# An AdaLN feed-forward kernel on one Trainium2 core: LoRA merge by three products of split operands, transfers and the first tile's y in another order

## The chip, the cores and the metric

The kernel runs on one core of one Trainium2 chip. The metric is the device time of one execution in microseconds (us), median of several runs. PE is TensorE, PEld its weight loads, DVE VectorE, ACT ScalarE, POOL GpSimd, SP the engine that here only issues transfers.

## The reference: what is computed

`x` holds 32 samples of 64 channels by 1024 values. Two residual layers follow each other:

```python
# layer 0: a 64x64 matrix per sample, chosen by its id, then a linear layer with eight LoRA adapters merged
y = jnp.einsum('bct,bcd->bdt', x, L0_cond_weights[itok_B_0_15])
h = jnp.einsum('bsd,nrd->nbsr', y, lora_A)                       # 8 adapters of rank 16
lora_out = jnp.einsum('nbsr,nor->bso', h, lora_B * (2 * lora_weights)[:, None, None])
x = x + jnp.einsum('bsd,od->bso', y, W) + bias + lora_out         # W is 1024 x 1024
# layer 1: a rank 16 adapter chosen by the sample's id, then a gated unit with 4-bit weights
v = jnp.einsum('bnr,bor->bno', jnp.einsum('bni,bri->bnr', x, B[ids]), A[ids])
inter = silu(v @ Wg.T) * (v @ Wu.T)                               # 2752 wide, weights from codes and scales
x = x + inter @ Wd.T
```

## The kernel before

The 2048 rows of `x` are 16 tiles of 128. All data is float32. Where a product has to be fast, both operands are split into a high part of the type fp32r and the rest (hi, lo), and three products are summed: hi by hi, hi by lo, lo by hi. An fp32r product of 512 columns is one pass on PE; a plain float32 product is shown in the trace as two records. The 4-bit codes of the second layer's weights are decoded all through the kernel: for each unit of 128 by 1024 codes ACT makes eight lines (L521, L525) in a ring of five buffers, DVE merges them into `val` in seven steps (L692, L694), multiplies by the scales (L711), PE turns the result (`turn_unit`), and ACT takes it out of PSUM (`evac_unit`).

Each engine's program is written out by hand and runs in its order; semaphores join them. Three stages follow each other:

**Setup** (0 to 48 us). The LoRA adapters are merged into W: We = W + B A, eight columns `jc` of 128 inputs. SP's queue loads the first unit's codes (`load_codes(0)`), then the eight columns of W with other inputs between them. ACT's queue loads `lb` (LoRA B), `lw` (the adapter weights) and `la` (LoRA A), all with the semaphore `lora_in`. DVE waits for all three, scales `lb` and puts it in order as `lbq`; PE turns it into `ps_t`; ACT copies it to `lbt`, which lies in the third buffer of `xs` (L586). Per column PE turns W (`turn_w`, eight transposes, L861) into one of two PSUM buffers (`ps_z` and `ps_gu` in turn, a column waits until the column two before it has been taken out) and adds the LoRA product with two plain float32 matmuls (`add_lora`, L866). ACT then writes `we_hi` (`evac_w`, L582) and DVE `we_lo` (`low_w`, L720). Between these stand decode work: ACT does 2 lines before each of the first four `evac_w` and 1 before the others, DVE 2 steps before each of the first two `low_w` and 1 before the others. After column 6 PE makes y of the first tile (`cond_y(0)`). After column 7 ACT takes y out (`evac_y`, both halves), DVE makes its low part (`low_y`, L744, both halves), and PE starts the tiles when `we_lo_ready` has counted all eight columns.

**Phase A** (16 tiles). Per tile PE computes z = y We by two halves of the output, each in two parts of four columns of y (`ffn_z`, L886, 12 matmuls a part), the y of the next tile, the turned sum x1 of the tile before (`turn_x1`, L895), the products of the adapters, and one or two turned units. The order in tile 0 is: z half 0 (both parts), y of tile 1, `turn_unit` of unit 0, z half 1 part 0, a bias product, `adapter_ga` of unit 0, z half 1 part 1, `turn_unit` of unit 1, then tile 1 with z half 0 part 0 and `turn_x1(0)`. DVE does in tile 0: 4 decode steps, `sum_x1` of half 0 (L751), 5 steps, `low_y` of tile 1's first half, 2 steps with the bias copy between them, then `low_y` of the second half and `sum_x1` of half 1, for which `turn_x1(0)` waits. ACT does 7 lines, `evac_unit(0)`, 2 lines, `evac_y`, 2 lines, `evac_ga(0)`, `evac_unit(1)` and then `evac_y` of tile 1's second half.

**Groups.** Six groups of hidden chunks, 16 slots each, compute the gated unit and add to the output in DRAM by accumulating transfers from POOL.

The functions below are those that the change touches and their callers.

Of the kernel before, what the change touches and what calls it, by code (L numbers as in the profile page):

```python
# [51 lines left out]
def adaln_ffn(nc, x, cond_id, adapter_id, cond_w, lora_a, lora_b, w0, bias0, lora_w, ad_a, ad_b,  # L52
# [3 lines left out]
    P = 128  # L56
# [90 lines left out]
    with ExitStack() as ctx:  # L147
# [52 lines left out]
        lbq = wt[:, 1, :, :]  # L200
        lbt = xs[:, XS - 1, :]
        ad_araw = x1t[:, :, :]
# [17 lines left out]
        ad_ids_in = sem("ad_ids_in")  # L220
        lora_in = sem("lora_in")
        ad_b_in = sem("ad_b_in")
# [18 lines left out]
        ad_at_ready = sem("ad_at_ready")  # L241
        lb_scaled = sem("lb_scaled")
        setup_t = sem("setup_t")
        setup_evac = sem("setup_evac")
# [84 lines left out]
        def _(sp):  # L329
# [20 lines left out]
            def load_x(t):  # L350
                slot = t % XS
                if t == XS - 1:
                    sp.wait_ge(we_mm, DC)
                elif t >= XS:
                    sp.wait_ge(x1t_mm, t - XS + 1)
                    sp.wait_ge(x1_out[slot], 16 * (t // XS))
                sp.dma_start(xs[:, slot, :], x_rows[t * P:(t + 1) * P, :]).then_inc(x_in[slot], 16)
# [5 lines left out]
            def load_w(jc):  # L363
                sp.dma_start(w_stage[jc][:, :, :], w0.rearrange("(q p) j -> p q j", p=P)[:, :, jc * P:(jc + 1) * P]
                             ).then_inc(w_in[jc], 16)

            load_codes(0)
            for jc in range(3):
                load_w(jc)
            sp.dma_start(ad_braw[:, :], ad_b.rearrange("n r d -> (n r) d")).then_inc(ad_b_in, 16)  # L370
# [139 lines left out]
        def _(act):  # L510
            act.dma_start(lb, lora_b.rearrange("n (p q) r -> p n (q r)", p=P)).then_inc(lora_in, 16)
            act.dma_start(lw[:, :], lora_w.partition_broadcast(P)).then_inc(lora_in, 16)
            act.dma_start(la[:, :], lora_a.rearrange("n r d -> (n r) d")).then_inc(lora_in, 16)
            def line(n, k):
# [65 lines left out]
            def evac_w(jc):  # L580
                act.wait_ge(we_mm, jc + 1)
                act.activation(we_hi[:, jc, :], ps_w[jc % 2][:, :], ACT.Copy).then_inc(we_hi_ready, 1)  # L582

            some_lines(0, 3)
            act.wait_ge(setup_t, 1)
            act.activation(lbt.rearrange("j (p q) -> j q p", q=DC),  # L586
                           ps_t[:, :].rearrange("j (q p) -> j q p", q=DC), ACT.Copy).then_inc(setup_evac, 1)
            at = 3
            for jc in range(DC):
                some_lines(at, 2 if jc < 4 else 1)  # L590
                at += 2 if jc < 4 else 1
                evac_w(jc)
                if jc == 4:
                    act.wait_ge(setup_t, 2)
                    act.wait_ge(ad_at_ready, 1)
                    act.activation(ad_bt[:, :, :].rearrange("p q t -> p (q t)"), ps_t[:, :], ACT.Copy
                                   ).then_inc(setup_evac, 1)
            evac_y(0, 0)
            evac_y(0, 1)
            some_lines(at, 1)  # L600
# [75 lines left out]
        def _(dve):  # L676
# [62 lines left out]
            def low_y(t, part):  # L739
                qs = slice(part * DC // 2, (part + 1) * DC // 2)  # L740
                dve.wait_ge(y_hi_ready, 2 * t + part + 1)
                if t == 0:
                    dve.wait_ge(we_mm, DC)
                dve.tensor_tensor(y_lo[:, qs, :].rearrange("p q t -> p (q t)"), ps_y[:, part * HALF:(part + 1) * HALF],  # L744
# [8 lines left out]
            def mask_bx(t):  # L753
# [6 lines left out]

            dve.wait_ge(lora_in, 16 * 3)
            dve.tensor_scalar(lw[:, :], lw[:, :], LORA_SCALE, None, ALU.mult).then_inc(lw_ready, 1)
# [3 lines left out]
            dve.tensor_copy(lbq.rearrange("p q (n r) -> p q n r", n=NAD),  # L766
                            lb.rearrange("p n (q r) -> p q n r", q=DC)).then_inc(lb_scaled, 1)
            some_steps(0, 2)
            at = 2
            for jc in range(DC):  # L770
                some_steps(at, 2 if jc < 2 else 1)
                at += 2 if jc < 2 else 1
                low_w(jc)
                if jc == 3:
                    dve.wait_ge(ad_a_in, 16)
                    dve.tensor_copy(ad_at[:, :, :, :], ad_araw.rearrange("p n (q r) -> p q n r", q=DC)
                                    ).then_inc(ad_at_ready, 1)
# [8 lines left out]
            assert at == STEPS_SETUP  # L786
            low_y(0, 0)
            low_y(0, 1)
            dve.wait_ge(mask_step, 3)

# [65 lines left out]
        def _(pe):  # L856
# [7 lines left out]
            def add_lora(jc):  # L864
                for h in range(2):
                    ins = pe.matmul(ps_w[jc % 2][:, h * HALF:(h + 1) * HALF], la[:, jc * P:(jc + 1) * P],  # L866
                                    lbt[:, h * HALF:(h + 1) * HALF], start=False, stop=True)
                ins.then_inc(we_mm, 1)
# [10 lines left out]
            def ffn_z(t, h, part):  # L879
                half = slice(h * HALF, (h + 1) * HALF)  # L880
                pe.wait_ge(y_lo_ready, 2 * t + part + 1 if h == 0 else 2 * (t + 1))
                if part == 0:
                    wait(pe, x1_ready, 2 * (t - 1) + h + 1)
# [54 lines left out]
            turn_w(1)  # L938
            pe.wait_ge(setup_evac, 1)
            add_lora(0)  # L940
# [12 lines left out]
            pe.wait_ge(ad_at_ready, 1)  # L953
            pe.wait_ge(we_lo_ready, DC)
            for t in range(NT):
# [104 lines left out]
```

## Time and profile before

| | us |
|---|---|
| median of 3 runs | 1100.68 (1100.24 to 1100.74) |
| the profiled execution's own time | 1100.7 |
| its span, first to last instruction | 1099.0 |
| PE busy | 1026.5 (93%) |
| DVE busy, ACT busy | 813.6 (74%), 806.4 (73%) |
| setup, until the first z matmul | 47.9 |
| end of phase A's last z matmul | about 356 |

The views of the profile give for each instruction its start and duration on its engine, and the idle time before it with what ended that. A group "x3" is several instructions run together. The granted clock (PEclk) is the share of TensorE's full clock in a stretch: 1.00 is 2.4 GHz, 0.50 is 1.2 GHz.

### The profile page before, as it was taken

What the parts mean: (1) busy time and instruction counts of PE and PEld (TensorE: products, weight loads), DVE (VectorE), ACT (ScalarE), POOL (GpSimd) and SP (SyncE); (2) the same over time, 40 slices, a digit from 0 to 9 for tenths busy, and PEclk for the clock granted to TensorE, in tenths of its full rate; (3) what the DMA queues carried; (4) which work ended last, traced back from release to release, by engine and by line L of the source; (5) the groups of instructions that cost most, each with busy time, mean ns of one, the idle gap of its engine ahead of it and who ended that gap; (6) DMA issues with size and microseconds to landing.
All of it is one profiled execution on the core that took longest, in us unless ns stands there. A gap on an engine that the chain in (4) does not pass through costs nothing.

```text
span 1099.0 us, 14511 instructions
## 1 busy us (share of the span) xinstructions
PE 1026.5 (93%) x5352; PEld 861.5 (78%) x5352; DVE 813.6 (74%) x815; ACT 806.4 (73%) x961; POOL 213.1 (19%) x285
## 2 busy tenths in 40 slices
PE   4899999999999889899999999999989999899995
PEld 3588888988888767778778778787878877788884
DVE  4778887878787788778888888888887788871220
ACT  4767777776677788878888888888888888863341
POOL 4003223232221111111111111121111211122111
PEclk9899999999999998999999999999999999999998
DMA  9735444464342366565645446455554645534667
GB/s 245 220 96 137 102 124 116 109 154 110 85 98 58 58 115 111 100 115 96 115 82 92 96 96 115 97 95 96 102 100 87 116 80 103 106 58 68 107 114 115
DMA packets 62950, 117.89 MB, mean 107 GB/s; under 512 B 6272, under 2 KB 38544, under 8 KB 62880
## 3 DMA queue, kind: packets, MB, share of 16 engines
q0 software_dynamic: 17504, 59.80, 34.7%
q1 hardware_dynamic: 44048, 56.11, 17.7%
q10 hardware_dynamic: 1328, 1.05, 0.3%
q8 instruction: 43, 0.70, 0.3%
q14 instruction: 27, 0.22, 0.1%
HBM read 58.22 MB, written 67.11 MB: 114 GB/s over the span
## 4 chain that ended last, share of the span: by engine, by line
PE 54%; DVE 24%; ACT 10%; issue 9%; SPq 2%; DMA 1%; DVEq 0%; POOL 0%; ACTq 0%
DVE val L692 12%; PE ps_z L1009 12%; PE ps_y L1009 11%; PE ps_z L886 10%; PE ps_gu L991 6%; DVE val L694 5%; ACT ring L525 5%; PE ps_t L928 3%; PE ps_t L920 3%; PE ps_gu L928 3%; ACT inter L629 2%; PE ps_y L875 2%; PE ps_gu L903 2%; DVE val L711 1%; DVE wd_late_lo L736 1%
## 5 line engine op out<-in xcount | busy, mean ns | idle before, releaser
L525 ACT ACTIVATE ring<-codes 128x1024 f32<-128x1024 int32 x455 | 455.4, 1053 | 119.2 <-DVE val L692 114.5
L692 DVE TENSOR_TENSOR val<-val,ring 128x1024 f32<-128x1024 f32 x260 | 318.1, 1223 | 15.2 <-issue 0.2
L694 DVE SCALAR_TENSOR_TENSOR val<-ring,val 128x1024 f32<-128x1024 f32 x195 | 238.0, 1220 | 11.1 <-ACT ring L525 2.5
L819 DVE TENSOR_TENSOR inter<-ps_gu,inter 128x512 f32<-128x512 f32 x88 | 60.7, 690 | 149.6 <-ACT inter L629 149.6
L497 POOL DMA_DIRECT2D out<-staged x96 | 82.6, 860 | 379.0 <-ACT staged L643 375.1
L886 PE MATMUL ps_z<-we_hi,y_hi 128*128 128x512 f32 x256 | 105.5, 412 | 3.6 <-DVE y_lo L744 3.6
L886 PE MATMUL ps_z<-we_hi,y_lo 128*128 128x512 f32 x256 | 101.1, 395 | 0.0
L886 PE MATMUL ps_z<-we_lo,y_hi 128*128 128x512 f32 x256 | 100.9, 394 | 0.0
L629 ACT ACTIVATE inter<-ps_gu 128x512 f32<-128x512 f32 x88 | 51.7, 587 | 62.9 <-PE ps_gu L991 62.3
L920 PE MATMUL ps_t<-ident,val 128*128 128x128 f32 x520 | 70.9, 280 | 20.0 <-DVE val L711 19.1
L1009 PE MATMUL ps_y<-wd_late_hi,in_hi 128*128 128x512 f32 x256 | 82.1, 402 | 6.9 <-DVE in_lo L825 5.5
L920 PEld LDWEIGHTS ps_t<-ident,val 128*128 128x128 f32 x520 | 64.5, 175 | 30.1 <-DVE val L711 24.5
L436 POOL TENSOR_TENSOR st_hi<-ga_f,one 128x128 fp32r<-128x128 f32 x42 | 28.7, 683 | 294.3 <-ACT ga_f L565 294.1
L1009 PE MATMUL ps_z<-wd_late_hi,in_hi 128*128 128x512 f32 x256 | 81.1, 398 | 0.0
L635 ACT ACTIVATE in_hi<-inter 128x512 fp32r<-128x512 f32 x88 | 55.5, 631 | 34.3 <-DVE inter L819 34.3
L521 ACT ACTIVATE val<-codes 128x1024 f32<-128x1024 int32 x65 | 68.7, 1057 | 9.1 <-PE ps_t L920 4.8
L1009 PE MATMUL ps_y<-wd_late_lo,in_hi 128*128 128x512 f32 x240 | 74.7, 393 | 0.0
L1009 PE MATMUL ps_y<-wd_late_hi,in_lo 128*128 128x512 f32 x240 | 74.5, 392 | 0.0
L1009 PE MATMUL ps_z<-wd_late_lo,in_hi 128*128 128x512 f32 x240 | 74.1, 390 | 0.0
L1009 PE MATMUL ps_z<-wd_late_hi,in_lo 128*128 128x512 f32 x240 | 74.0, 389 | 0.0
L991 PE MATMUL ps_gu<-bx_hi,st_hi 128*128 128x512 f32 x176 | 69.6, 395 | 3.5 <-DVE inter L819 3.5
L991 PE MATMUL ps_gu<-bx_hi,st_lo 128*128 128x512 f32 x176 | 69.6, 395 | 0.0
(117 smaller groups left out, 1829.8 us busy)
## 6 DMA issues: line engine op xcount, KB each, us to landing
out<-staged POOLq DMA_DIRECT2D x96, 512.0 KB, 5.3
codes<-in_L_ffn_gate_codes SPq DMA_DIRECT2D x21, 512.0 KB, 3.5
codes<-in_L_ffn_up_codes SPq DMA_DIRECT2D x21, 512.0 KB, 3.7
codes<-in_L_ffn_down_codes SPq DMA_DIRECT2D x21, 512.0 KB, 4.0
xs<-in_x SPq DMA_DIRECT2D x16, 512.0 KB, 3.6
out<-in_L_ffn_bias SPq DMA_DIRECT2D x4, 2048.0 KB, 13.2
out<-xs POOLq DMA_DIRECT2D x16, 512.0 KB, 5.5
w_stage<-in_L_ffn_W SPq DMA_DIRECT2D x8, 512.0 KB, 9.9
```

What stands on the lines that cost most here:

```text
L497: pool.dma_start(out_rows[t * P:(t + 1) * P, :], staged[:, place, :], accum_op=ALU.add).then_inc(acc_out[place], 16)
L521: act.activation(val_of(n), codes[:, n % 2, :], ACT.Relu, bias=offset, scale=slope).then_inc(lines, 1)
L525: act.activation(ring[:, (k - 1) % RING, :], codes[:, n % 2, :], ACT.Identity, bias=offset, scale=slope).then_inc(lines, 1)
L629: act.activation(inter[:, q % 2, :], ps_g[:, :], ACT.Silu).then_inc(silu_ready, 1)
L692: ins = dve.tensor_tensor(v, v, line, pick)
L694: ins = dve.scalar_tensor_tensor(out=v, in0=line, scalar=add, in1=v, op0=ALU.add, op1=pick)
L819: dve.tensor_tensor(inter[:, q % 2, :], ps_u[:, :], inter[:, q % 2, :], ALU.mult).then_inc(inter_ready, 1)
L886: ins = pe.matmul(ps_z[:, half], y[:, jc, :], w[:, jc, half], start=jc == 0 and p == 0, stop=jc == DC - 1 and p == 2)
L920: ins = pe.transpose(ps_t[:, q * P:(q + 1) * P], v[:, q, :], ident[:, :])
L928: ins = pe.matmul(ga_bank(n), ad_at[:, q, :, :].rearrange("p n r -> p (n r)"), wt[:, m % 2, q, :], start=q == 0, stop=q == DC - 1)
L991: ins = pe.matmul(ps, w[:, c % ST, m, :], v[:, cols], start=p == 0, stop=p == 2)
L1009: ins = pe.matmul(ps_o[slot % 2][:, h * HALF:(h + 1) * HALF], v[:, b % 2, k, s * P:(s + 1) * P], wd_of(c, w)[:, h * HALF:(h + 1) * HALF], ...
```

## The change

- `lbt` and `la` are split into hi and lo parts. These lie in `bx_hi` and `bx_lo`, which phase A fills later; `lbt` leaves `xs`. ACT makes `la_hi` (a copy as soon as `la` has come) and `lbt_hi`, both ahead of its first three decode lines. DVE makes `la_lo` and `lbt_lo` ahead of its first two decode steps. `add_lora` takes six fp32r matmuls of 512 columns in place of two float32 ones, and PE waits for both low parts.
- DVE's first wait is for `lb` and `lw` alone; `la` has a semaphore of its own.
- SP loads columns 0 and 1 of W ahead of the first codes. The third tile's x no longer waits for the end of the merge.
- ACT's `evac_y` of tile 0 stands ahead of the last `evac_w`, DVE's `low_y` ahead of the last `low_w`, without its wait for the last column. PE starts z when seven columns of `we_lo` are done, and waits for the eighth ahead of each part 1.

```diff
@@ -198,7 +198,8 @@
 
         lb = wt[:, 0, :, :].rearrange("p (n q) r -> p n (q r)", n=NAD)
         lbq = wt[:, 1, :, :]
-        lbt = xs[:, XS - 1, :]
+        lbt_hi, la_hi = bx_hi[:, 0:D], bx_hi[:, D:2 * D]
+        lbt_lo, la_lo = bx_lo[:, 0:D], bx_lo[:, D:2 * D]
         ad_araw = x1t[:, :, :]
 
         in_hi = sb("in_hi", [P, 2, IN, HALF], F32R)
@@ -218,7 +219,8 @@
 
         ids_in = sem("ids_in")
         ad_ids_in = sem("ad_ids_in")
-        lora_in = sem("lora_in")
+        lora_a_in = sem("lora_a_in")
+        lora_b_in = sem("lora_b_in")
         ad_b_in = sem("ad_b_in")
         ad_a_in = sem("ad_a_in")
         bias_in = sem("bias_in")
@@ -240,6 +242,8 @@
         lw_ready = sem("lw_ready")
         ad_at_ready = sem("ad_at_ready")
         lb_scaled = sem("lb_scaled")
+        la_hi_ready = sem("la_hi_ready")
+        lora_lo_ready = sem("lora_lo_ready")
         setup_t = sem("setup_t")
         setup_evac = sem("setup_evac")
         we_mm = sem("we_mm")
@@ -349,9 +353,7 @@
 
             def load_x(t):
                 slot = t % XS
-                if t == XS - 1:
-                    sp.wait_ge(we_mm, DC)
-                elif t >= XS:
+                if t >= XS:
                     sp.wait_ge(x1t_mm, t - XS + 1)
                     sp.wait_ge(x1_out[slot], 16 * (t // XS))
                 sp.dma_start(xs[:, slot, :], x_rows[t * P:(t + 1) * P, :]).then_inc(x_in[slot], 16)
@@ -364,9 +366,10 @@
                 sp.dma_start(w_stage[jc][:, :, :], w0.rearrange("(q p) j -> p q j", p=P)[:, :, jc * P:(jc + 1) * P]
                              ).then_inc(w_in[jc], 16)
 
+            load_w(0)
+            load_w(1)
             load_codes(0)
-            for jc in range(3):
-                load_w(jc)
+            load_w(2)
             sp.dma_start(ad_braw[:, :], ad_b.rearrange("n r d -> (n r) d")).then_inc(ad_b_in, 16)
             load_w(3)
             sp.dma_start(ad_araw.rearrange("p (n q) r -> p n (q r)", n=NAD),
@@ -508,9 +511,9 @@
 
         @block.scalar
         def _(act):
-            act.dma_start(lb, lora_b.rearrange("n (p q) r -> p n (q r)", p=P)).then_inc(lora_in, 16)
-            act.dma_start(lw[:, :], lora_w.partition_broadcast(P)).then_inc(lora_in, 16)
-            act.dma_start(la[:, :], lora_a.rearrange("n r d -> (n r) d")).then_inc(lora_in, 16)
+            act.dma_start(lb, lora_b.rearrange("n (p q) r -> p n (q r)", p=P)).then_inc(lora_b_in, 16)
+            act.dma_start(lw[:, :], lora_w.partition_broadcast(P)).then_inc(lora_b_in, 16)
+            act.dma_start(la[:, :], lora_a.rearrange("n r d -> (n r) d")).then_inc(lora_a_in, 16)
             def line(n, k):
                 if n >= NU:
                     return
@@ -581,22 +584,25 @@
                 act.wait_ge(we_mm, jc + 1)
                 act.activation(we_hi[:, jc, :], ps_w[jc % 2][:, :], ACT.Copy).then_inc(we_hi_ready, 1)
 
+            act.wait_ge(lora_a_in, 16)
+            act.activation(la_hi, la[:, :], ACT.Copy).then_inc(la_hi_ready, 1)
+            act.wait_ge(setup_t, 1)
+            act.activation(lbt_hi.rearrange("j (p q) -> j q p", q=DC),
+                           ps_t[:, :].rearrange("j (q p) -> j q p", q=DC), ACT.Copy).then_inc(setup_evac, 1)
             some_lines(0, 3)
-            act.wait_ge(setup_t, 1)
-            act.activation(lbt.rearrange("j (p q) -> j q p", q=DC),
-                           ps_t[:, :].rearrange("j (q p) -> j q p", q=DC), ACT.Copy).then_inc(setup_evac, 1)
             at = 3
             for jc in range(DC):
                 some_lines(at, 2 if jc < 4 else 1)
                 at += 2 if jc < 4 else 1
+                if jc == DC - 1:
+                    evac_y(0, 0)
+                    evac_y(0, 1)
                 evac_w(jc)
                 if jc == 4:
                     act.wait_ge(setup_t, 2)
                     act.wait_ge(ad_at_ready, 1)
                     act.activation(ad_bt[:, :, :].rearrange("p q t -> p (q t)"), ps_t[:, :], ACT.Copy
                                    ).then_inc(setup_evac, 1)
-            evac_y(0, 0)
-            evac_y(0, 1)
             some_lines(at, 1)
             at += 1
             assert at == LINES_AT[0]
@@ -739,8 +745,6 @@
             def low_y(t, part):
                 qs = slice(part * DC // 2, (part + 1) * DC // 2)
                 dve.wait_ge(y_hi_ready, 2 * t + part + 1)
-                if t == 0:
-                    dve.wait_ge(we_mm, DC)
                 dve.tensor_tensor(y_lo[:, qs, :].rearrange("p q t -> p (q t)"), ps_y[:, part * HALF:(part + 1) * HALF],
                                   y_hi[:, qs, :].bitcast(F32).rearrange("p q t -> p (q t)"), ALU.subtract
                                   ).then_inc(y_lo_ready, 1)
@@ -758,18 +762,28 @@
                                          in1=mask[:, PER * t:PER * (t + 1)].unsqueeze(2).to_broadcast([P, PER, CH]),
                                          op0=ALU.add, op1=ALU.mult).then_inc(bx_masked, 1)
 
-            dve.wait_ge(lora_in, 16 * 3)
+            dve.wait_ge(lora_b_in, 16 * 2)
             dve.tensor_scalar(lw[:, :], lw[:, :], LORA_SCALE, None, ALU.mult).then_inc(lw_ready, 1)
             dve.wait_ge(lw_ready, 1)
             dve.tensor_tensor(lb, lb, lw[:, :].unsqueeze(2).to_broadcast([P, NAD, P]), ALU.mult).then_inc(lw_ready, 1)
             dve.wait_ge(lw_ready, 2)
             dve.tensor_copy(lbq.rearrange("p q (n r) -> p q n r", n=NAD),
                             lb.rearrange("p n (q r) -> p q n r", q=DC)).then_inc(lb_scaled, 1)
+            dve.wait_ge(la_hi_ready, 1)
+            dve.tensor_tensor(la_lo, la[:, :], la_hi.bitcast(F32), ALU.subtract).then_inc(lora_lo_ready, 1)
+            dve.wait_ge(setup_evac, 1)
+            dve.tensor_tensor(lbt_lo.rearrange("j (p q) -> j q p", q=DC),
+                              ps_t[:, :].rearrange("j (q p) -> j q p", q=DC),
+                              lbt_hi.bitcast(F32).rearrange("j (p q) -> j q p", q=DC), ALU.subtract
+                              ).then_inc(lora_lo_ready, 1)
             some_steps(0, 2)
             at = 2
             for jc in range(DC):
                 some_steps(at, 2 if jc < 2 else 1)
                 at += 2 if jc < 2 else 1
+                if jc == DC - 1:
+                    low_y(0, 0)
+                    low_y(0, 1)
                 low_w(jc)
                 if jc == 3:
                     dve.wait_ge(ad_a_in, 16)
@@ -784,8 +798,6 @@
             dve.wait_ge(ad_ids_in, 16)
             dve.tensor_scalar(mask[:, :], ad_ids[:, :], part_f[:, 0:1], None, ALU.is_equal).then_inc(mask_step, 1)
             assert at == STEPS_SETUP
-            low_y(0, 0)
-            low_y(0, 1)
             dve.wait_ge(mask_step, 3)
 
             for t in range(NT):
@@ -863,8 +875,10 @@
 
             def add_lora(jc):
                 for h in range(2):
-                    ins = pe.matmul(ps_w[jc % 2][:, h * HALF:(h + 1) * HALF], la[:, jc * P:(jc + 1) * P],
-                                    lbt[:, h * HALF:(h + 1) * HALF], start=False, stop=True)
+                    half = slice(h * HALF, (h + 1) * HALF)
+                    for p, (a, b) in enumerate(((la_hi, lbt_hi), (la_hi, lbt_lo), (la_lo, lbt_hi))):
+                        ins = pe.matmul(ps_w[jc % 2][:, half], a[:, jc * P:(jc + 1) * P], b[:, half],
+                                        start=False, stop=p == 2)
                 ins.then_inc(we_mm, 1)
 
             def cond_y(t):
@@ -879,6 +893,8 @@
             def ffn_z(t, h, part):
                 half = slice(h * HALF, (h + 1) * HALF)
                 pe.wait_ge(y_lo_ready, 2 * t + part + 1 if h == 0 else 2 * (t + 1))
+                if part == 1:
+                    pe.wait_ge(we_lo_ready, DC)
                 if part == 0:
                     wait(pe, x1_ready, 2 * (t - 1) + h + 1)
                 for jc in range(part * DC // 2, (part + 1) * DC // 2):
@@ -936,7 +952,7 @@
                 ins = pe.transpose(ps_t[:, q * P:(q + 1) * P], lbq[:, q, :], ident[:, :])
             ins.then_inc(setup_t, 1)
             turn_w(1)
-            pe.wait_ge(setup_evac, 1)
+            pe.wait_ge(lora_lo_ready, 2)
             add_lora(0)
             add_lora(1)
             for jc in range(2, DC):
@@ -951,7 +967,7 @@
                     cond_y(0)
             pe.wait_ge(setup_evac, 2)
             pe.wait_ge(ad_at_ready, 1)
-            pe.wait_ge(we_lo_ready, DC)
+            pe.wait_ge(we_lo_ready, DC - 1)
             for t in range(NT):
                 a, b, b_before = PLACE_A[t, 0], PLACE_A.get((t, 1)), PLACE_A.get((t - 1, 1))
                 ffn_z(t, 0, 0)
```

## Rows read from the trace of the kernel before

**Rows 1.** The page, part 1: busy time, share of the span, instructions of each engine.

```profile
PE 1026.5 (93%) x5352; PEld 861.5 (78%) x5352; DVE 813.6 (74%) x815; ACT 806.4 (73%) x961; POOL 213.1 (19%) x285
```

**Rows 2.** Stretches: length, busy time (count) by engine, PEclk, DMA share, GB/s.

```profile
24.00:36.00 12.00, 10.50 (x52) 6.28 (x51) 9.48 (x10) 9.21 (x10) 0.00 (x0) 1.00 1.10 319
...
44.00:48.00 4.00, 0.42 (x2) 0.16 (x1) 2.55 (x6) 3.31 (x5) 0.00 (x0) 0.81 0.32 121
...
48.00:54.00 6.00, 6.00 (x16) 4.70 (x17) 5.13 (x5) 3.60 (x4) 0.00 (x0) 0.56 0.48 175
...
80.00:120.00 40.00, 40.00 (x248) 35.54 (x247) 34.31 (x35) 30.49 (x36) 11.01 (x16) 1.00 0.58 144
```

**Rows 3.** The chain that ended last, 0 to 120 us: start, us, what.

```profile
19.46 8.60 DMA codes<-in_L_ffn_up_codes
...
30.09 1.23 DVE we_lo L720
...
31.46 1.06 PE ps_z L861 x8
...
32.52 1.72 PE ps_z L866 x4
...
42.57 1.73 PE ps_gu L866 x4
...
47.87 8.23 PE ps_z L886 x24
...
86.27 5.46 PE ps_z L886 x24
```

**Rows 4.** Timeline, setup: start, us, engine line op out<-in [idle before <-what ended it].

```profile
11.92 1.94 PE L861 MATMUL ps_z<-ident,w_stage 128*128 128x128 f32 x8 [11.92 <-DMA w_stage<-in_L_ffn_W]
...
12.56 0.17 DVE L762 TENSOR_SCALAR lw<-lw 128x8 f32<-128x8 f32 x1 [12.56 <-DMA la<-in_L_ffn_lora_A]
...
16.78 2.04 ACT L586 ACTIVATE xs<-ps_t 128x1024 f32<-128x1024 f32 x1 [8.44 <-PE ps_t L936]
...
18.87 2.10 PE L866 MATMUL ps_z<-xs,la 128*128 128x512 f32 x4 [0.42 <-ACT xs L586]
...
35.77 1.22 DVE L720 TENSOR_TENSOR we_lo<-ps_z,we_hi 128x1024 fp32r<-128x1024 f32 x1
```

**Rows 5.** Transfers issued at 0.87 (codes) and 1.78 us (W column 1): KB, us to landing.

```profile
codes<-in_L_ffn_gate_codes SPq DMA_DIRECT2D x1, 512.0 KB, 4.5
...
w_stage<-in_L_ffn_W SPq DMA_DIRECT2D x1, 512.0 KB, 14.4
```

**Rows 6.** Timeline, end of setup and tile 0.

```profile
47.04 1.28 DVE L744 TENSOR_TENSOR y_lo<-ps_y,y_hi 128x512 fp32r<-128x512 f32 x2
...
47.63 1.06 ACT L521 ACTIVATE val<-codes 128x1024 f32<-128x1024 int32 x1 [0.37 <-DMA codes<-in_L_ffn_gate_codes]
...
52.15 1.23 DVE L711 TENSOR_TENSOR val<-val,gu_scales 128x1024 f32<-128x1024 f32 x1
...
56.75 3.87 DVE L694 SCALAR_TENSOR_TENSOR val<-ring,val 128x1024 f32<-128x1024 f32 x3
...
66.41 1.06 ACT L525 ACTIVATE ring<-codes 128x1024 f32<-128x1024 int32 x1 [0.29 <-DVE val L692]
...
68.76 1.03 ACT L537 ACTIVATE wt<-ps_t 128x1024 f32<-128x1024 f32 x1 [1.12 <-PE ps_t L920]
...
71.64 1.09 PE L895 MATMUL ps_t<-ident,xs 128*128 128x128 f32 x8 [0.17 <-DVE xs L751]
```

**Rows 7.** Timeline of PE in the groups, where it stood idle before a step.

```profile
624.35 1.16 PE L920 MATMUL ps_t<-ident,val 128*128 128x128 f32 x8 [2.10 <-DVE val L711]
...
714.45 2.90 PE L928 MATMUL ps_t<-wt,ad_at 128*128 128x128 f32 x16 [1.87 <-ACT wt L537]
```

**Rows 8.** Stretches around these two.

```profile
624.00:628.00 4.00, 3.65 (x20) 3.07 (x20) 3.17 (x4) 4.00 (x6) 0.00 (x0) 1.00 0.03 4
...
714.00:720.00 6.00, 5.55 (x25) 4.97 (x26) 5.86 (x7) 5.35 (x8) 0.06 (x1) 0.72 0.32 87
```

## The prediction

> **What bounds the kernel now.** First the page's busy times: PE works 93% of the span and no other engine over 74% [rows 1], so time is won where PE stands still or runs slowly. The stretches tell where. In phase A PE is busy 40.00 of 40 us at the upper clock, DVE 34.31 [rows 2]; PE bounds it, and whatever moves the start of the tiles moves the end. From 44 to 48 us PE works only 0.42 us, and from 48 to 54 its granted clock is 0.56 on the mean [rows 2]: the hole at the end of setup and the lower of the two levels (1.2 GHz) behind it. Third, the chain of waits: the last LoRA product ends at 44.30 (42.57 and 1.73), ACT and DVE finish the last column and then make the low part of y, and z starts at 47.87 [rows 3]. Its first 24 matmuls take 8.23 us where 24 later ones take 5.46 [rows 3]. So 3.57 us are a wait and 2.77 us the clock after it. I call the end of the last LoRA product L; before, L is 44.30.
>
> The same chain shows what holds the front of setup: the second unit's codes, issued at 19.46, land 8.60 later at 28.06. ACT then makes one line and `evac_w(2)`, DVE's `low_w(2)` follows at 30.09, and column 4 is turned at 31.46 [rows 3]. Everything earlier is worth only what it does to this.
>
> **The front of setup: gains nothing.** DVE started at 12.56, when `la` came [rows 4]; now `lb` and `lw` free it. But three other things come later. Ahead of the first lines ACT has `la_hi` (not before 12.6; about 1.03 by [rows 6], ACT at 68.76) and `lbt_hi` (2.04 [rows 4]), ending at about 15.7; it was idle 8.44 us here [rows 4], which pays for both. The first codes now stand third on SP's queue, behind 1 MB of W. Before, the third transfer there (column 1 of W) landed 14.4 us after its issue at 1.78, so at 16.2, and the codes at 5.4 [rows 5]. The same three transfers in another order put the codes at no later than about 16.2; I take 16.2. ACT then does five lines (1.06 each [rows 6]) to 21.5, `evac_w(0)` (1.03 like the eviction there) to 22.5, two lines, `evac_w(1)` to 25.7 and line 7 to 26.7: 1.3 us before the codes that it needs next, which keep their place behind the same bytes on the same queue. DVE has `la_lo` (1.22 as [rows 4], DVE at 35.77) and `lbt_lo`. The trace has no DVE write with that step: at least 1.22, and if the step doubles it as it doubled ACT's (2.04 against 1.03) 2.44; I take 1.22, the same operation. Either end is over by 18.3, when DVE's first step gets its second line, so it costs nothing. From 18.3 DVE does four steps, `low_w(0)`, two steps, `low_w(1)` and a step: 7 times 1.23 and 2 times 1.22 [rows 4, 6] give 29.4, against `low_w(2)` at 30.09. So column 4 is again turned at about 31.5, with 0.7 us to spare on DVE. If the first codes or `la` come more than that later, each us beyond is a us on L.
>
> **The columns: 0 to 1.4 us.** `add_lora` falls from 1.72 [rows 3] to six matmuls of 5.46/24 = 0.228 each, 1.37: 0.35 less per column. Not all of it counts: for columns 5 and 6 PE waits for DVE, whose `low_w(4)` starts at 35.77 because DVE comes from other work [rows 4]. That leaves columns 6 and 7: L = 44.30 - 0.70 = 43.6 (bounds: nothing, 44.3; all of columns 4 to 7, 42.9). Against it stands the clock. PE now ends `add_lora(1)` by 20 to 22 us and must wait for `low_w(0)` until about 24.4, so a hole of 2 to 4 us. Holes in this trace: 3.57 us was followed by the lower level [rows 2, 3], 1.87 too, 2.10 was not [rows 7, 8]. At the lower level column 2 takes 1.94 (eight transposes at 11.92 [rows 4]) and twice 1.37, so to 29.1, and column 4 is turned 1.4 us later; of that about 0.65 reaches L, as the columns behind have slack in their waits for DVE. With even chances I put L at **43.9** (43.6 to 44.3).
>
> A rule speaks against this part. The chain has eight transposes per column at 1.06 with the clock up from 24 to 36 us [rows 2, 3]; and after nothing but transposes since 11.92 the first LoRA matmuls at 18.87 ran nearly at the rate of later ones (2.10 for four against 1.72) [rows 3, 4]. The Trainium skill, "TensorE: Matmul & The Clock Gate", Part 4, says that in transpose mode the full clock does not engage, as it doesn't count as PE-busy in the same way. By that rule, with less matmul time between the transposes, the merge would run at the lower level; the trace disagrees, since transposes alone brought the clock up. What this would cost is the slower rival below.
>
> **The end of setup: the main gain, and what is late next.** `evac_y` and `low_y` now finish while PE turns and merges the last column, so z can start at L + 0.1, with PE never idle and the clock up. The wait for the eighth column ahead of part 1 is met: `evac_w(7)` and `low_w(7)` take 1.03 and 1.22 after L [rows 4, 6], 2.3 with their handoffs, and part 0 has 12 matmuls, 2.73. In later tiles this wait is met long before; it costs 32 satisfied waits, and where z's parts with one and two waits follow each other now, 24 matmuls run at 0.228 without a step [rows 3], so nothing. If PE alone counted, it would come to `turn_x1(0)` 0.1 + (71.64 - 0.17 - 47.87 - 2.77) = 20.9 us after L [rows 3, 6].
>
> But DVE and ACT are next. `turn_x1(0)` needs `sum_x1`, which stands behind all of DVE's and ACT's work of tile 0. Before, from L to `turn_x1(0)` it was 71.64 - 44.30 = 27.34 [rows 3, 6]. Out of this falls: `low_y`, moved ahead of L, 1.28 (at 47.04); DVE's wait for z, from 53.38 (52.15 and 1.23) to 56.10 (47.87 and 8.23), 2.72; and ACT's wait for PE ahead of `evac_unit(1)`, 1.12 [rows 3, 6]. The rest stays, for it is DVE steps back to back (from 56.75 to 66.41, where ACT's line waits for the last of them) and then ACT, DVE and PE in turn. I add 0.3, because ACT's seven lines, one eviction and two lines in tile 0 now end a little after DVE wants the y behind them (0 to 1). So 27.34 - 1.28 - 2.72 - 1.12 + 0.3 = 22.5 after L: 1.6 later than PE alone. Of the third unit's codes ACT has use at 47.63, their landing [rows 6]; its next line then waits for DVE until about L + 5.2 = 49.1, so this isn't the limit while L is above 43.5.
>
> **The sum.** `turn_x1(0)` comes at 43.9 + 22.5 = 66.4 instead of 71.64: 5.2 us. At that point all engines stand to each other as before (ACT behind `evac_y`, DVE behind `sum_x1`), and every later wait is for another engine or a transfer issued by one, so the shift stays. The profiled execution took 1100.7, as the median does (1100.68): **1095.5**. The bounds of L (42.9 to 44.3) and of the 0.3 give 1093.8 to 1096.6.
>
> **The rivals.** (a) DVE is not next, or does its tile 0 quicker than here: PE's path alone, 43.9 + 20.9 = 64.8, gain 6.8, 1093.9. For it: PE's 93% [rows 1]; against: the steps back to back. (b) One more fall of the clock. PE gets a new hole of about 1.6 us at `turn_x1(0)`, and the holes in the groups move against the clock's decisions: 1.87 cost a fall, 2.10 did not [rows 7, 8]. One fall costs about what it did at 48 us, 2.77 [rows 3]: 1098.3. (c) The same luck the other way, one fall fewer: 1092.7. (d) The front is late by more than its slack, by some 3 to 5 us (first codes or `la` landing late, so that ACT and DVE lag): L is 47 to 49 and the gain 0 to 2: 1099 to 1101, the case in which the moves only shift the wait. (e) Slower: the whole merge at the lower clock level, because transposes with shorter products between them, or the holes ahead of each column, let it stay down. A column is then 1.94 + 2.74 = 4.7 [rows 3, 4]; six from 24.4, with the adapter's eight transposes and the 16 records of y between them (three times 1.94, an estimate), put L at 58.4, 14.1 later than before, and the 4.9 won behind L shrink to about 3.5 as z starts slowly too: 1100.7 + 10.6 = 1111. The page's rule would have it so. It decides from L = 71.64 - 22.5 = 49.1 on, that is when more than about two and a half columns behind column 3 run so, each 2.3 us over. Against it: at the lower level PE is itself the last to finish, without holes, and after 47.87 the clock came back within six us of work [rows 2].
>
> **How the numbers follow.** The forecast 0.52, (a) 0.10, (b) 0.15, (c) 0.10, (d) 0.08, (e) 0.05. A measurement of this kernel can tell about 0.2%, 2.2 us, from no change. Faster by that (under 1098.5): the forecast, (a), (c) and over half of (b), 0.83. Slower: (e), 0.05. Within: 0.12. A range from 1092.2 to 1098.8 holds the forecast, (a), (c) and most of (b), and leaves (d) and (e) out.
>
> **What will show it.** Column 4 turned at about 31.5 (up to 33 with the clock down); the merge's end at 43.6 to 44.3; the first z within 0.3 us of it, and its 24 matmuls in 5.5 us; `turn_x1(0)` near 66.4 with PE idle about 1.5 us before it, released by DVE; from there a constant shift against the kernel before. It is wrong if z waits for `y_lo` or the eighth column, if the first codes land after 17 us and column 4 moves with them, if the clock is down beyond 33 us, or if the shift changes in the groups.

## The result and the profile after

The changed kernel took 1094.19 us (median of five runs, 1092.53 to 1096.04) against 1100.68 us: a ratio of 0.9943, 95% interval 0.9929 to 0.9958. The forecast was 1095.5. The profiled execution took 1094.19, with a span of 1092.5.

The chain of waits of the kernel after, in order of time (start, us, what), answers to [rows 3]:

```profile
18.61 8.93 DMA codes<-in_L_ffn_up_codes
...
36.60 1.07 PE ps_z L873 x8
...
41.72 1.40 PE ps_gu L880 x6
...
64.66 0.61 DVE xs L755
...
65.31 1.09 PE ps_t L911 x8
```

The second unit's codes still hold the front: they land at 27.54, before at 28.06. The six matmuls of a column take 1.40 (four records of float32 took 1.72). The merge ends at L = 41.72 + 1.40 = 43.12, before at 44.30. `turn_x1(0)` is now at 65.31 instead of 71.64, released by DVE.

The timeline shows the front, z's start and the end of tile 0 (start, us, instruction, in brackets the idle time before it and what ended it), beside [rows 4, 6]:

```profile
10.78 1.06 ACT L588 ACTIVATE bx_hi<-la 128x1024 fp32r<-128x1024 f32 x1 [6.87 <-DMA la<-in_L_ffn_lora_A]
...
14.79 2.01 DVE L775 TENSOR_TENSOR bx_lo<-ps_t,bx_hi 128x1024 fp32r<-128x1024 f32 x1 [1.69 <-ACT bx_hi L590]
...
15.10 1.06 ACT L524 ACTIVATE val<-codes 128x1024 f32<-128x1024 int32 x1 [0.34 <-DMA codes<-in_L_ffn_gate_codes]
...
17.14 3.89 DVE L700 SCALAR_TENSOR_TENSOR val<-ring,val 128x1024 f32<-128x1024 f32 x3 [0.33 <-ACT ring L528]
...
23.63 1.94 PE L873 MATMUL ps_z<-ident,w_stage 128*128 128x128 f32 x8 [2.42 <-DVE we_lo L726]
...
27.34 1.04 PE L873 MATMUL ps_gu<-ident,w_stage 128*128 128x128 f32 x8
...
27.56 1.06 ACT L524 ACTIVATE val<-codes 128x1024 f32<-128x1024 int32 x1 [2.96 <-DMA codes<-in_L_ffn_up_codes]
...
30.93 1.06 PE L873 MATMUL ps_z<-ident,w_stage 128*128 128x128 f32 x8 [0.29 <-DVE we_lo L726]
...
43.26 0.47 PE L902 MATMUL ps_z<-we_hi,y_hi 128*128 128x512 f32 x1
...
58.10 0.68 DVE L748 TENSOR_TENSOR y_lo<-ps_y,y_hi 128x512 fp32r<-128x512 f32 x1
...
65.31 1.09 PE L911 MATMUL ps_t<-ident,xs 128*128 128x128 f32 x8 [0.96 <-DVE xs L755]
```

The stretches at the end of setup (length, busy time by engine, granted clock, DMA) answer to the middle rows of [rows 2]:

```profile
44.00:48.00 4.00, 4.00 (x19) 3.27 (x18) 3.59 (x6) 2.19 (x3) 0.00 (x0) 1.00 0.51 164
...
48.00:54.00 6.00, 6.00 (x40) 5.41 (x39) 5.76 (x6) 5.15 (x6) 0.00 (x0) 1.00 0.21 81
```

PE is busy 4.00 of 4 us where it had 0.42, and the clock is 1.00 where it was 0.81 and 0.56. z starts 0.14 us after the merge. What is left of the hole is the 0.96 us of idle PE ahead of `turn_x1(0)`, and DVE ends it.

Behind `turn_x1(0)` the two profiles take the same time: the span's end comes 1092.5 - 65.31 = 1027.2 us later, before 1099.0 - 71.64 = 1027.4. So the shift of 6.3 us made in setup and tile 0 is the whole difference of the two spans but 0.2. That they agree so closely is partly chance: in the other profiles below this stretch takes 1026.3 to 1029.0 us.

### The profile page after: what moved, and what is told of

It reads as the page before. It is cut to its first block, busy times and chain, and to the rows that moved or that the text cites. A ratio compares the mean times of both kernels' runs of the same rounds, so it can differ in the third digit from the quotient of the medians.

```text
span 1092.5 us, 14576 instructions
## 1 busy us (share of the span) xinstructions
PE 1023.8 (94%) x5368; PEld 864.8 (79%) x5368; DVE 816.8 (75%) x817; ACT 807.1 (74%) x962; POOL 213.1 (20%) x285
## 4 chain that ended last, share of the span: by engine, by line
PE 52%; DVE 26%; ACT 10%; issue 9%; SPq 2%; DMA 1%; DVEq 0%; POOL 0%; ACTq 0%
DVE val L698 13%; PE ps_z L1025 12%; PE ps_y L1025 11%; PE ps_z L902 9%; PE ps_gu L1007 6%; DVE val L700 6%; ACT ring L528 5%; PE ps_t L944 3%; PE ps_t L936 3%; PE ps_gu L944 3%; ACT inter L635 2%; PE ps_gu L919 2%; PE ps_y L889 2%; DVE val L717 2%; DVE wd_late_lo L742 1%
```

## Experiments

All were timed beside the kernel before on the same chip; there that kernel's medians were 1099.0 to 1100.3. T is the start of `turn_x1(0)`, L the end of the last LoRA product, both from each run's own profile.

| kernel | L | T | T - L | median us | ratio, 95% interval |
|---|---|---|---|---|---|
| before (first profile) | 44.30 | 71.64 | 27.3 | 1100.68 | |
| before again | 44.68 | 69.50 | 24.8 | 1099.06 | 0.9994 [0.9984, 1.0005] |
| after (first profile) | 43.12 | 65.31 | 22.2 | 1094.19 | 0.9943 [0.9929, 0.9958] |
| after again | 42.82 | 65.01 | 22.2 | 1094.07 | 0.9953 [0.9939, 0.9966] |
| y early alone | 44.50 | 66.70 | 22.2 | 1095.50 | 0.9962 [0.9947, 0.9976] |
| all but y early | 43.21 | 69.65 | 26.4 | 1097.86 | 0.9983 [0.9973, 0.9993] |
| codes first | 43.63 | 65.83 | 22.2 | 1094.77 | 0.9960 [0.9944, 0.9975] |
| before, clock held | 44.78 | 69.61 | 24.8 | 1098.28 | 0.9989 [0.9978, 1.0000] |
| after, hole filled | 44.71 | 66.90 | 22.2 | 1094.62 | 0.9952 [0.9938, 0.9965] |
| after, a step moved | 42.61 | 64.08 | 21.5 | 1091.15 | 0.9922 [0.9909, 0.9936] |
| after, masks early | 42.99 | 64.53 | 21.5 | 1093.01 | 0.9937 [0.9924, 0.9951] |
| after, both of these | 42.99 | 64.45 | 21.5 | 1091.81 | 0.9926 [0.9912, 0.9939] |
| after, ten steps in four tiles | 43.54 | 65.03 | 21.5 | 1090.97 | 0.9911 [0.9896, 0.9927] |

**One part alone.** The y split early, in the kernel before:

```diff
+                if jc == DC - 1:
+                    evac_y(0, 0)
+                    evac_y(0, 1)
                 evac_w(jc)
...
-                if t == 0:
-                    dve.wait_ge(we_mm, DC)
...
+                if jc == DC - 1:
+                    low_y(0, 0)
+                    low_y(0, 1)
                 low_w(jc)
...
+                if part == 1:
+                    pe.wait_ge(we_lo_ready, DC)
...
-            pe.wait_ge(we_lo_ready, DC)
+            pe.wait_ge(we_lo_ready, DC - 1)
```

> The kernel before with only the split y moved ahead of the last column (ACT, DVE and PE's two waits); LoRA stays in float32, transfers in their old order. Theory: the merge ends at 44.3 as before, z starts within 0.2 us of it at the upper clock, turn_x1(0) follows 22.2 us after the merge's end at 66.5 instead of 71.64, and the time falls by 5.1 us to about 1095.6. Rival (DVE is not next, PE alone sets tile 0): turn_x1(0) at 65.2, 1094.3. Rival (the gain is the cheaper merge's): 1100.7.

The changed kernel without that part (the same diff, undone):

> The changed kernel with the split y back behind the last column; split LoRA and the new transfers stay. Theory: the merge ends at 43.1, the hole of 3.6 us and the lower clock behind it come back, turn_x1(0) at 43.1 + 27.3 = 70.4, so 1.2 us under the kernel before: 1099.5. Rival (the merge's gain is lost because the second unit's codes and DVE set the columns): 1100.7. Rival (the split merge carries most of the gain): under 1097.

The chain of the first of them, and then of the second:

```profile
42.77 1.73 PE ps_gu L866 x4
...
66.70 1.09 PE ps_t L897 x8
```

```profile
41.82 1.39 PE ps_gu L880 x6
...
46.79 7.33 PE ps_z L900 x24
...
69.65 1.09 PE ps_t L909 x8
```

With y early alone the merge ends where it did, and T - L falls to 22.2: T stands at 66.70 where 66.5 was expected, not at the 65.2 of PE alone. Without it, L has its gain and the hole is back (z 3.58 us after L). So y early shortens what comes behind the merge, and the rest of the change moves the merge's end by about 1.2 us. Measured end to end, all but y early brought 1.2 us, as expected, and y early alone 3.5, not 5.1. The next experiment shows a reason: executions of the kernel before differ, and T of y early alone lies 4.9 us below the T of its first profile and 2.8 below that of its second.

**The clock by itself.** Fifteen matmuls that nobody reads are to hold the clock in the hole of the kernel before:

```diff
+            for _ in range(15):
+                pe.matmul(ps_t[:, 0:HALF], we_hi[:, 0, 0:P], we_hi[:, 0, 0:HALF], start=True, stop=True)
             pe.wait_ge(we_lo_ready, DC)
```

> The kernel before with 15 matmuls of 512 columns, whose result nobody reads, in the hole at the end of setup; z still waits for y and the last column until 47.9. Theory: the clock stays at its upper level, the first 24 z matmuls take 5.5 us instead of 8.2, and turn_x1(0) comes 2.8 us earlier (PE sets it: DVE's wait for z of 2.7 us goes): 1097.9. Rival (only the wait counts, the slow start hides beside DVE's steps): 1100.7.

And a second profile each of the two kernels, unchanged:

> The kernel before, for a second profile. Theory: turn_x1(0) at 71.6 if the clock is down for all of the first 13 z matmuls as in the first profile, up to 1 us earlier if it comes back sooner; the time behind turn_x1(0) is 1027 us as in every profile so far. Rival (the stages behind also differ from run to run by 1 us or more without the clock): another time behind it.

> The changed kernel, for a second profile and a comparison on one chip with the others. Theory: the merge's end at 43.1 to 43.6, turn_x1(0) 22.2 us later, 1027 us behind it; 5 to 6.3 us shorter than the kernel before on the same chip. Rival (the profile of the changed kernel was a lucky one): turn_x1(0) at 66.4 or later, 4 us or less.

The chain of the kernel with the clock held, then chain and stretches of the kernel before in its second profile:

```profile
48.36 5.72 PE ps_z L886 x24
...
69.61 1.09 PE ps_t L895 x8
```

```profile
48.25 5.72 PE ps_z L886 x24
...
69.50 1.09 PE ps_t L895 x8
...
44.00:48.00 4.00, 0.66 (x2) 0.00 (x0) 2.17 (x5) 3.15 (x5) 0.00 (x0) 1.00 0.29 107
...
48.00:54.00 6.00, 5.75 (x26) 4.81 (x27) 5.50 (x6) 3.40 (x4) 0.00 (x0) 1.00 0.52 175
```

With the fifteen matmuls z's first 24 take 5.72 instead of 8.23, and T - L is 24.8, 2.5 less than in the first profile (2.8 were expected). But the unchanged kernel shows the same 5.72 and the same 24.8 in its second profile: a hole as long as before (3.57 us), and no fall of the clock behind it (1.00, where [rows 2] have 0.81 and 0.56). So whether the clock falls in this hole differs from one execution to the next; behind the hole of 3.58 us in the kernel with all but y early it did fall (z took 7.33). That the fifteen matmuls hold the clock is therefore not shown by their profile; in the median they brought 0.8 us, and the interval reaches no difference. The times of the kernel before spread in the same sense: of its 26 executions beside this run, the three with a mean granted clock of 0.982 took 1102.5 to 1103.0 us, the two with 0.988 took 1097.6 and 1097.9. In which stretches these had the lower clock is not known. What y early takes out of T - L is 2.6 us in either case (24.8 to 22.2) and about 2.5 more in those executions in which the clock falls. From the second profile of before to the second of after T moves by 4.5 us, from the first to the first by 6.3.

Such a difference between executions stands behind T too. The second profile of the changed kernel has T at 65.01, but from there to the end it takes 1.8 us longer, and one stretch accounts for 1.6 of that. First the first profile, then the second, each with PE's next step behind the hole:

```profile
353.00:367.00 14.00, 11.56 (x64) 9.43 (x65) 8.77 (x12) 9.90 (x13) 0.86 (x2) 1.00 0.19 35
...
365.12 0.70 PE L1025 MATMUL ps_y<-wd_late_hi,in_hi 128*128 128x512 f32 x2 [1.33 <-DVE wd_late_lo L742]
```

```profile
353.00:367.00 14.00, 11.68 (x59) 9.81 (x60) 7.33 (x10) 8.71 (x12) 0.86 (x2) 0.88 0.17 33
...
366.40 0.70 PE L1025 MATMUL ps_y<-wd_late_hi,in_hi 128*128 128x512 f32 x2 [1.54 <-DVE wd_late_lo L742]
```

The last `turn_x1` comes at 353.41 and 353.09, with 1.08 us of idle PE before it and 0.70 behind it in both, and the step at the end of the stretch 11.7 and 13.3 us later: the clock fell in one and not in the other, for 1.6 us. In all profiles the time from T to the end is 1026.3 to 1029.0 us where the tiles' work is as in the kernel before; the tiles between, from the first `turn_x1` to the last, take 288.1 in both profiles of both kernels.

**The transfers' order.** The first codes ahead of W again:

```diff
+            load_codes(0)
             load_w(0)
             load_w(1)
-            load_codes(0)
             load_w(2)
```

> The changed kernel with the first codes again ahead of columns 0 and 1 of W. Theory: column 0 lands at 11.8 instead of 5.7, so the turned LoRA B and its split come some 2.7 us later, and with them ACT's lines and DVE's steps; 1.35 us of that are slack on DVE ahead of low_w(2), the rest, 1 to 1.4 us, goes on to the merge's end: 1095.2 to 1095.6. Rival (the front is all slack, the second unit's codes set it): 1094.2.

L is 43.63, 0.5 to 0.8 later than in the two profiles of the changed kernel. But L also moves with the landing of the second unit's codes, and that has to be taken out first. In six profiles of the new merge (six matmuls of split operands a column) ACT stands idle over 2 us until they land, and in each of them L comes 15.54 to 15.56 us after the start of ACT's first line on them (27.56 and 43.12 in the changed kernel's first profile). In the four profiles of the old merge it is 16.21 to 16.22 (28.09 and 44.30 in the first). So these codes set L, and the cheaper merge is worth 16.21 - 15.55 = 0.66 us; what else L gains is that they land earlier, with that line at 27.07 to 28.00 against 28.09 to 28.57. Why they do stays open. In this run:

```profile
27.67 1.06 ACT L524 ACTIVATE val<-codes 128x1024 f32<-128x1024 int32 x1 [0.80 <-DMA codes<-in_L_ffn_up_codes]
```

ACT is idle for 0.80 us only, and L is 15.96 behind: the old order costs 0.4 us on L. The theory had 1 to 1.4. The medians (1094.77 against 1094.07 and 1094.19) don't show a difference of this size.

**The hole ahead of column 2.** Sixteen matmuls that nobody reads, behind `add_lora(1)`:

```diff
             add_lora(1)
+            for _ in range(16):
+                pe.matmul(ps_t[:, 0:HALF], la_hi[:, 0:P], lbt_hi[:, 0:HALF], start=True, stop=True)
```

> The changed kernel with 16 matmuls of 512 columns, whose result nobody reads, in the hole ahead of column 2. Theory: the clock no longer falls there (0.50 from 24 to 26 us in the changed kernel), columns 2 and 3 take their short time, but the merge still ends at 43.1 to 43.3, since the second unit's codes at 27.6 and DVE set column 4: no difference in the median, though the spread of the runs may be smaller. Rival (the fall of the clock ahead of column 2 costs time on the path in most runs): 0.6 us or more shorter than the changed kernel beside it.

```profile
13.22 1.06 ACT L588 ACTIVATE bx_hi<-la 128x1024 fp32r<-128x1024 f32 x1 [9.31 <-DMA la<-in_L_ffn_lora_A]
...
23.62 4.18 PE L959 MATMUL ps_t<-bx_hi 128*128 128x512 f32 x16
...
27.63 1.04 PE L873 MATMUL ps_z<-ident,w_stage 128*128 128x128 f32 x8
...
33.02 1.04 PE L873 MATMUL ps_z<-ident,w_stage 128*128 128x128 f32 x8
```

This didn't test what it should. The filler held column 2 until 27.63, and ACT stood idle 2.12 us until it was merged; besides, `la` came 2.4 us later here than in the first profile. Column 4 was turned at 33.02 and L is 44.71. Two kernels of the next experiments settle what this one left open. In the one with the masks early `la` was as late (13.40), and L is 15.93 us behind ACT's line on the second unit's codes, 0.4 over the 15.55. Here it is 17.79 behind, 2.2 over, so most of that is the filler's own. And in the kernel with both changes the hole was 1.34 us long, and column 2's transposes ran at the upper rate behind it:

```profile
23.58 1.07 PE L873 MATMUL ps_z<-ident,w_stage 128*128 128x128 f32 x8 [1.34 <-DVE we_lo L726]
...
27.44 1.06 ACT L524 ACTIVATE val<-codes 128x1024 f32<-128x1024 int32 x1 [2.89 <-DMA codes<-in_L_ffn_up_codes]
```

Its L is 42.99, 15.55 behind that line, as in the changed kernel, where column 2's transposes ran at the lower rate (1.94). So the lower clock behind the hole ahead of column 2 costs nothing on L: even with it column 3's transposes start at 27.34, and the codes that ACT needs next land at 27.54, after them.

**What is next in tile 0.** One decode step and line of tile 0 goes to tile 12:

```diff
-    STEPS_A = [11 if t < 12 else 10 for t in range(NT)]
+    STEPS_A = [11 if 0 < t < 13 else 10 for t in range(NT)]
```

> The changed kernel with one of the 11 decode steps and lines of tile 0 moved to tile 12. Theory (DVE's steps of tile 0 set turn_x1(0), PE stands idle 0.96 us before it): the step of 1.23 us leaves the path, PE's idle time there falls to a few hundredths, and turn_x1(0) comes 0.9 us earlier, 64.4 with the merge's end at 43.1; the run is 0.9 us shorter than the changed kernel beside it. Rival (that idle time is covered elsewhere, or PE or ACT's eviction of unit 1 is next at the same point): no difference.

The three steps for the masks, to where DVE waits for `la_hi` (and, in another kernel, both changes):

```diff
+            dve.wait_ge(part_ready, 1)
...
+            dve.tensor_scalar(mask[:, :], ad_ids[:, :], part_f[:, 0:1], None, ALU.is_equal).then_inc(mask_step, 1)
             dve.wait_ge(la_hi_ready, 1)
```

> The changed kernel with the three small DVE steps of the masks (0.64 us from the end of low_w(7) to the first decode step of tile 0) moved to the start of DVE's program, where it waits for la_hi. Theory (DVE sets tile 0): turn_x1(0) comes 0.6 us earlier against the merge's end, 21.6 us instead of 22.2, PE's idle time ahead of it falls from 0.96 to about 0.35 us, the time behind it stays at 1027. Rival (PE or ACT is next at once): 22.1 to 22.2.

> The changed kernel with both: one decode step of tile 0 moved to tile 12, and the masks early. Theory: PE alone now sets tile 0 (20.9 to 21.2 us from the merge's end to turn_x1(0) by its own work), so against the step alone, which gave 21.5, the masks bring 0.2 to 0.3 us and no more; about 1091. Rival (DVE still sets it): 20.9.

The step in front of which PE stood idle, in the timelines of these three in their order:

```profile
64.08 1.09 PE L911 MATMUL ps_t<-ident,xs 128*128 128x128 f32 x8 [0.24 <-DVE xs L755]
```

```profile
64.53 1.09 PE L911 MATMUL ps_t<-ident,xs 128*128 128x128 f32 x8 [0.20 <-DVE xs L755]
```

```profile
64.45 1.09 PE L911 MATMUL ps_t<-ident,xs 128*128 128x128 f32 x8 [0.24 <-DVE xs L755]
```

Each takes about 0.7 us from T - L (22.2 to 21.5), PE's idle time falls from 0.96 to 0.2, and both together bring no more than one. What stands behind DVE's steps is in the chain of the kernel with the step moved:

```profile
60.21 0.89 PE ps_t L936 x8
...
62.05 0.60 ACT y_hi L574
...
63.34 0.69 DVE xs L755
```

PE turns unit 1, ACT takes it and then y out of PSUM, DVE makes `low_y` (for which it stood idle 3.25 us) and `sum_x1`: this series ends at 21.5 us after L, and PE's own work ahead of `turn_x1(0)` ends 0.24 us before that. The expected 0.2 to 0.3 us more from both changes didn't come. The step moved was expected to bring 0.9 us and brought 2.9 (1094.07 to 1091.15 on one chip). 0.7 of that are in tile 0; in the profiles 1.7 are in the tiles behind, 286.4 us from the first `turn_x1` to the last instead of 288.1. To see whether that was DVE's lag, ten steps in the first four tiles, eleven in all others:

```diff
-    STEPS_A = [11 if t < 12 else 10 for t in range(NT)]
+    STEPS_A = [10 if t < 4 else 11 for t in range(NT)]
```

> The changed kernel with 10 decode steps in tiles 0 to 3 and 11 in all others, instead of 11 in tiles 0 to 11 and 10 behind. Theory for tile 0: as with one step moved, 21.5 us from the merge's end to turn_x1(0). For phase A, where moving one step took 1.7 us out of the 288.1 between the first and the last turn_x1, if that was DVE's lag in the tiles: 286.4 or less. Rival (the order of the units was luck): 287 to 289, since tiles 12 to 15 now have a step more.

```profile
65.03 1.09 PE L911 MATMUL ps_t<-ident,xs 128*128 128x128 f32 x8 [0.24 <-DVE xs L755]
...
350.89 1.06 PE L911 MATMUL ps_t<-ident,xs 128*128 128x128 f32 x8 [1.08 <-DVE wd_early_lo L742]
```

285.9 us between the two rows, 2.2 under 288.1, with more steps in the last tiles. So where the decode steps stand sets part of phase A's time. How it does is read from PE between the first `turn_x1` and the last: the stretch (length, PE's busy time) and PE's waits there for DVE's `sum_x1` (us in total, times, longest), for the changed kernel, the step moved and the ten steps:

```profile
65.31:353.41 288.10, 282.48 (x1762) 249.54 (x1763) 235.12 (x236) 206.99 (x243) 71.13 (x108) 1.00 0.47 112
...
PE ps_t L911 <- DVE xs L755: 3.9, 8, 1.0
```

```profile
64.08:350.44 286.36, 282.04 (x1762) 249.62 (x1763) 236.22 (x237) 209.45 (x245) 72.77 (x108) 1.00 0.47 113
...
PE ps_t L911 <- DVE xs L755: 2.4, 7, 0.6
```

```profile
65.03:350.89 285.86, 282.23 (x1763) 249.73 (x1763) 236.06 (x237) 209.86 (x245) 77.23 (x108) 1.00 0.48 113
...
PE ps_t L911 <- DVE xs L755: 1.3, 5, 0.4
```

PE stands idle 5.6 us in the changed kernel, 4.3 with the step moved, 3.6 with the ten steps, and its work stays the same within 0.5. The stretch from 80 to 120 us [rows 2], where PE was busy 40.00 of 40 us, is not typical of the phase: most of the gain is time in which PE waited for DVE ahead of a `turn_x1`. With 1090.97 us this kernel has the lowest median, but it can't be told from the step alone (0.9911 and 0.9922, with intervals that overlap). Its interval lies below both of the changed kernel's, that of the step alone below the one from the same chip (0.9953).

## Why the prediction was right, and where not

The way, the size and the place were as forecast: 1095.5 against 1094.19, T at 66.4 against 65.31, the shift constant behind it. Step by step:

- **The front gains nothing, the second unit's codes hold it.** Right in mechanism. Column 4 was turned at 30.93, not 31.5: the codes landed 0.5 earlier, which the sum had as unchanged. The first codes came at 15.1 (taken 16.2), `la` at 10.8 (not before 12.6). `lbt_lo` took 2.01, not the 1.22 that I chose between 1.22 and 2.44; it is hidden as argued, with DVE's first step waiting another 0.33 for ACT.
- **L.** Forecast 43.9, measured 43.12 and 42.82 in the two profiles. The 0.35 per column for two columns was right: 0.70, and 0.66 by the distance of L from the codes. The 0.3 that I put on L for the fall of the clock was wrong: the fall came (behind a hole of 2.42 us), but column 2 was still done before the codes landed, so it used slack that I had not credited to it, and the profile without the fall has the same distance. The rest is the codes' 0.5, which the sum did not foresee.
- **z.** It starts 0.14 us after L with the clock up, as forecast; the eighth column is never waited for.
- **DVE is next in tile 0.** 22.2 against 22.5. The idle time ahead of `turn_x1(0)` is there, 0.96 instead of 1.6 us, and DVE ends it; taking 0.6 to 1.2 us of DVE's work out of tile 0 shortens it until PE stands at 21.5. The 0.3 for ACT's lateness was too much: `low_y` starts at 58.10, as soon as DVE is free. And PE's own work takes 21.2 (21.5 less 0.24 of idle time), not the 20.9 that rival (a) was given; with ACT's and DVE's steps behind its last turned unit it is 21.5.
- **The clock behind the hole.** This is the step that failed in part. From one profile I took 2.77 us as a fixed cost of the hole. It is 2.5, since the first 24 z matmuls take 5.72 without a fall and not 5.46; and the second profile has the hole without the fall. The gain from y early is 2.6 us in either case, the rest comes only in executions in which the clock falls; so T moved by 4.5 to 6.3 us by profile, and the medians by 6.5 us in the first comparison and 5.2 in the later one (0.9953 of 1099.5). (b) and (c) had allowed for one fall more or less, but not for this one. That the forecast of 5.2 lies so near is partly luck: a fall counted as certain, which isn't, stands against 1.1 us that L and T - L gained beyond the sum.
- **The range.** Its lower bound for the sum, 1093.8, doesn't follow from its terms: L at 42.9 is 1.0 under the 43.9 and the 0.3 falls away, so 1094.2. The measured 1094.19 lies just there.
- **The rivals.** (a) is out by the y split alone (66.70, not 65.2) and by the four kernels that lighten DVE in tile 0. (d) is out, as the front has its slack, though the filled hole shows how it would have come. (e) is out: from column 3 on eight transposes take 1.04 to 1.07, and the granted clock is 1.00 from 28 to 54 us. The rule of the Trainium skill ("TensorE: Matmul & The Clock Gate", Part 4), that the full clock does not engage in transpose mode, isn't borne out in the merge. In the front the two profiles of the changed kernel differ: PE had done only transposes there, with holes between them, when the LoRA matmuls began; in the first profile these ran at half rate, in the second at the upper rate until a fall at about 17.4:

```profile
16.96 0.39 PE L880 MATMUL ps_z<-bx_lo,bx_hi 128*128 128x512 f32 x1
...
17.19 0.41 PE L880 MATMUL ps_z<-bx_hi,bx_lo 128*128 128x512 f32 x1
```

  These start 0.23 us apart, so the clock can be up after transposes alone. (b) was seen in the second profile of the changed kernel, at 355 us, where the groups begin, at 1.6 us instead of 2.77.
- **"PE bounds phase A"** was too strong: it was read from 40 us without a hole, and over the phase PE stands idle 5.6 us of 288.1. The shift argument holds without it, since tiles of the same order take the same time (288.1 in four profiles); but two placements of DVE's steps took 1.7 and 2.2 us out of phase A.

## What to carry to other kernels

A hole at the seam of two stages can be closed by moving the next stage's first inputs ahead of the last stage's tail; what the move is worth is found by walking the engine that becomes late next, here DVE with one tile's decode, and not by the idle time that PE shows. What the clock does behind a hole of a few microseconds can differ from execution to execution: take it from a second profile before it enters a sum as a fixed cost. Busy time in one short stretch doesn't say that an engine bounds a phase: take it from the whole phase. And a shift that leaves every later order alone arrived at the end here, within the 2.7 us by which the time behind T differs between profiles, so setup can be judged by the start of the first step that all engines share.

## What was not expected of the hardware

- DVE's subtraction with a stepped write and one stepped operand took 2.01 us against 1.22 for the same size without a step; ACT's stepped copy 2.02 against 1.03.
- The same hole, 3.57 us long in two executions of one kernel, was followed by the lower clock in one and not in the other; two of 1.08 and 0.70 us at 352 to 355 us were followed by it in one of two.
- In the first profile of the kernel after the granted clock is shown as 1.00 from the start, while the matmuls of the first columns ran at half rate:

```profile
17.45 0.63 PE L880 MATMUL ps_z<-bx_lo,bx_hi 128*128 128x512 f32 x1
...
17.88 0.63 PE L880 MATMUL ps_z<-bx_hi,bx_lo 128*128 128x512 f32 x1
...
20.60 0.39 PE L880 MATMUL ps_gu<-bx_lo,bx_hi 128*128 128x512 f32 x1
...
20.83 0.39 PE L880 MATMUL ps_gu<-bx_hi,bx_lo 128*128 128x512 f32 x1
```

Those at 17.45 and 17.88 start 0.43 us apart, those at 20.60 and 20.83 only 0.23, with 512 columns each. For the first 20 us of this profile the spacing of the matmuls tells the clock, the column doesn't.
